# Second attention: row maxima two pairs ahead, row sums in adds of 1024 columns on GpSimd

## The reference, cut to what matters

```
k_in = v_in = layer_norm(ctx) * g + b            # ctx: 8 x 1601 x 128
q = rope(q_in @ Wq + bq);  k = rope(k_in @ Wk + bk);  v = v_in @ Wv + bv     # 16 heads of 64
scores = einsum("bhqd,bhkd->bhqk", q, k) / 8;  keys past the length: -inf
attn = softmax(scores, axis=-1);  out = einsum("bhqk,bhkd->bhqd", attn, v)
x = x + tanh(g_xattn[1]) * (out.reshape(8, 256, 1024) @ Wo + bo)
```

## Time and profile before

| what | us |
|---|---|
| median of 3 runs | 3376.14 |
| lowest and highest | 3375.39, 3378.19 |
| the profiled execution, its own time | 3378.97 |
| its span, first to last instruction | 3377.2 |
| PE busy | 2960.7 |
| DVE busy | 2171.2 |
| ACT busy | 1449.0 |
| POOL busy | 1340.0 |

### The profile page before, as it was taken

One profiled execution on the slowest core, in us unless ns is written; L12 is line 12 of the kernel. 1 busy time (PEld: TensorE's weight loads), 2 busy tenths in 40 slices (PEclk: granted clock), 3 DMA queues, 4 the chain that ended last, 5 costly groups with the idle time before them and its releaser, 6 DMA issues. The chain is left out here.

```text
span 3377.2 us, 81656 instructions
## 1 busy us (share of the span) xinstructions
PE 2960.7 (88%) x32026; PEld 1721.3 (51%) x32026; DVE 2171.2 (64%) x6576; ACT 1449.0 (43%) x2171; POOL 1340.0 (40%) x1205
## 2 busy tenths in 40 slices
PE   4599999999999367589899898998989989995998
PEld 3444444444444245356556565665656656663454
DVE  4366666665664544677777777777777777774343
ACT  2256656665665022244444444444444444441211
POOL 2000000000000000378778787877878878783000
PEclk8789999998998578699999999999999999997999
DMA  4400000000000000200000000000000000001000
GB/s 126 134 20 14 14 14 13 14 14 14 14 10 2 25 0 0 87 6 16 11 6 23 6 16 11 7 22 6 16 11 8 21 6 7 8 3 43 0 0 13
DMA packets 66728, 66.16 MB, mean 20 GB/s; under 512 B 8543, under 2 KB 60271, under 8 KB 65860
## 3 DMA queue, kind: packets, MB, share of 16 engines
q1 hardware_dynamic: 66372, 61.18, 6.3%
HBM read 53.23 MB, written 7.92 MB: 18 GB/s over the span
## 5 line engine op out<-in xcount | busy, mean ns | idle before, releaser
L1383 ACT ACTIVATE a_probs<-psS 128x1024 f32<-128x1024 f32 (+1 forms) x448 | 431.7, 964 | 777.5 <-PE psS L1280 777.5
L648 DVE CUSTOM_DVE_ANT_0 a_junk<-psT,a_mask 128x384 f16<-128x384 f32 (+1 forms) x1024 | 547.8, 574 | 332.2 <-PE psT L528 318.3
L610 ACT ACTIVATE a_probs<-psS 128x1024 f32<-128x1024 f32 (+2 forms) x512 | 442.5, 864 | 240.0 <-PE psS L553 240.0
L1679 POOL MEMSET a_shut<- 128x3328 f16 x1 | 2.9, 2872 | 1312.8 <-POOLq L1082 1312.8
L1673 POOL TENSOR_TENSOR a_acc<-a_acc,a_probs 128x512 f32<-128x512 f32 x320 | 408.2, 1276 | 274.7 <-ACT a_probs L1383 273.0
L1675 POOL TENSOR_TENSOR a_acc<-a_acc,a_probs 128x512 f32<-128x512 f32 x320 | 407.4, 1273 | 25.1
L1524 DVE CUSTOM_DVE_ANT_0 a_junk<-psS,a_mask 128x400 f16<-128x400 f32 (+1 forms) x512 | 273.6, 572 | 106.0 <-PE psS L1255 89.0
L1524 DVE CUSTOM_DVE_ANT_0 a_junk<-psT,a_mask 128x400 f16<-128x400 f32 (+1 forms) x512 | 273.6, 572 | 100.5 <-PE psT L1255 84.5
L564 PE MATMUL psO<-a_probs,a_values 128*9 128x256 f32 x3328 | 325.3, 393 | 0.5 <-ACT a_turned L622 0.5
L543 PE MATMUL psS<-a_mask_t,a_stack 128*64 128x256 f16 x3328 | 292.2, 290 | 0.0
L1647 POOL TENSOR_TENSOR a_klo<-a_kt,a_khi 128x400 f16<-128x400 f32 (+1 forms) x256 | 242.7, 948 | 9.9 <-ACT a_khi L1424 9.9
(11 more groups left out here) (308 smaller groups left out, 5736.9 us busy)
## 6 DMA issues: line engine op xcount, KB each, us to landing
a_wq<-in_wq SPq DMA_DIRECT2D x64, 128.0 KB, 2.1
a_kaug<-a_keys SPq DMA_DIRECT2D x288, 24.0 KB
a_keys<-p_kst SPq DMA_DIRECT2D x8, 832.0 KB, 4.7
p_ctx<-in_ctx SPq DMA_DIRECT2D x8, 768.0 KB
a_ctx<-in_ctx SPq DMA_DIRECT2D x8, 768.0 KB
a_mask<-a_pad SPq DMA_DIRECT2D x8, 400.2 KB
a_kaug<-a_keys SPq DMA_DIRECT2D x96, 32.0 KB
p_mask_raw<-in_mask_t SPq DMA_DIRECT2D x6, 448.0 KB, 6.2
```

The source lines that it names most:

```text
L610: nc.scalar.activation(dst, src, ACT.Exp).then_inc(exp_done, 1)
L648: nc.vector.tensor_tensor_reduce(junk[:, i % 2, 0:PIECE[j]], psA[i % 2][:, 0:PIECE[j]], mask[:, t, j, 0:PIECE[j]], 1.0, LOWEST, ALU.add, A ...
L1383: nc.scalar.activation(dst, src, ACT.Exp).then_inc(exp_done, 1)
```

## The change

- Row maxima are taken two pairs ahead: `ahead` and `row_max` are for pair `it + 2`, with `AHEAD1` = 2, 2, 1, 1, 1, 1, 0 units in the slots. `negative_max` is in slot 6, `turn_max` and `take_max` in slot 1 of the next iteration.
- The keys and the query go three pairs ahead (`it + 3`), so four pairs are kept (`KEPT1`), and there is one more iteration at the start.
- POOL keeps the slot's two chunks apart in an accumulator of 128 x 1024, and so adds a whole slot in one instruction: five adds of 1024 columns and one of 512 for a pair.
- `total` makes one column per head and block of 128 queries: 16 fp32 matmuls with 64 columns of the accumulator as the stationary operand and one column of ones as the moving one. They are a piece of the ring, `sums`. DVE takes the reciprocal of these four columns (`invert_sums`). `spread` in slot 4 spreads them over 64 rows by four matmuls with the identity, ACT copies the result to SBUF (`take_inverse`), and `divide` only multiplies, in slot 5.
- The statistics of a context are spread over the slots of the iteration before, the normalising is split into four groups in slots 1 to 4, the transposes are in slots 2 to 5. ACT makes the fp16 high part from PSUM, and DVE's `context_hi` is gone.
- `project` and `leave` stand behind `weigh`.

```diff
-AHEAD1 = [2, 2, 2, 2, 0, 0, 0]
+AHEAD1 = [2, 2, 1, 1, 1, 1, 0]
+KEPT1 = 4
 RING1 = 5
 VALUES1 = {2: (0, 1), 4: (2, 3)}
-ITERATIONS1 = range(-2, PAIRS1 + 1)
+ITERATIONS1 = range(-3, PAIRS1 + 1)
...
+        w.acc = sb("a1_acc", [P, 2, 4, T])
+        w.rec, w.inv = sb("a1_rec", [P, 2, 2, TT]), sb("a1_inv", [P, 2, T])
...
             def total(n):
-                pe.wait_ge(sum_done, SLOTS1 * (n + 1))
+                pe.wait_ge(sum_done, 6 * (n + 1))
+                out = piece(("sums", n))
                 for hd in range(2):
-                    ins = nc.tensor.matmul(w.sums[n % 2][64 * hd:64 * hd + 64, T:2 * T], m.ones[:, 0:64],
-                                           w.acc[:, n % 2, hd, :], start=True, stop=True, skip_group_check=True)
+                    for t in range(TT):
+                        for part in range(2):
+                            o = t * P + 64 * part
+                            for x in range(2):
+                                ins = nc.tensor.matmul(out[64 * part:64 * part + 64, hd * TT + t:hd * TT + t + 1],
+                                                       w.acc[:, n % 2, 2 * hd + x, o:o + 64], m.ones[:, 0:1],
+                                                       start=(hd == 0 and t == 0 and x == 0), stop=(x == 1),
+                                                       skip_group_check=True)
+                ins.then_inc(near_full, 1)
+
+            def spread(n):
+                pe.wait_ge(rec_done, n + 1)
+                for t in range(TT):
+                    for hd in range(2):
+                        ins = nc.tensor.matmul(w.sums[n % 2][64 * hd:64 * hd + 64, T + t * P:T + (t + 1) * P],
+                                               w.rec[:, n % 2, hd, t:t + 1].to_broadcast([P, 64]), m.ident[:, :],
+                                               start=False, stop=True, skip_group_check=True)
                 ins.then_inc(r_full, 1)
...
-                    if is_pair(it + 1):
+                    if is_pair(it + 2):
                         for u in units_ahead(sl):
                             for hd in range(2):
-                                ahead(it + 1, u, hd)
-                    if normed_in(it) is not None and 1 <= sl <= 4:
-                        turn(normed_in(it), sl - 1)
+                                ahead(it + 2, u, hd)
+                    if normed_in(it) is not None and 2 <= sl <= 5:
+                        turn(normed_in(it), sl - 2)
                     if is_pair(it + 1):
                         for v in VALUES1.get(sl, ()):
                             value(it + 1, v)
-                    if is_pair(it + 2) and sl == 3:
-                        query(it + 2)
-                    if is_pair(it + 2) and sl >= 3:
+                    if is_pair(it + 3) and sl == 3:
+                        query(it + 3)
+                    if is_pair(it + 3) and sl >= 3:
                         for part in range(2):
-                            key(it + 2, sl - 3, part)
-                    if leaves_in(it) is not None and sl == 5:
-                        project(leaves_in(it))
-                    if leaves_in(it) is not None and sl == 6:
-                        leave(leaves_in(it))
+                            key(it + 3, sl - 3, part)
+                    if is_pair(it + 1) and sl == 1:
+                        turn_max(it + 1)
                     if sl == 0 and is_pair(it - 1):
                         weigh(it - 1, SLOTS1 - 1)
                     if sl > 0 and is_pair(it):
                         weigh(it, sl - 1)
                     if sl == 3 and is_pair(it - 1):
                         total(it - 1)
-                    if sl == 5 and is_pair(it + 1):
-                        turn_max(it + 1)
+                    if sl == 4 and is_pair(it - 1):
+                        spread(it - 1)
+                    if leaves_in(it) is not None and sl == 5:
+                        project(leaves_in(it))
+                    if leaves_in(it) is not None and sl == 6:
+                        leave(leaves_in(it))
...
+                if nb >= 2:
+                    act.wait_ge(near_full, at["value", PER_BATCH * (nb - 1) - 1, 3] + 1)
+                nc.scalar.activation(w.chi[:, nb % 2, o:o + width], src[:, 0:width], ACT.Identity, bias=w.shift[:, :],
+                                     scale=w.gain[:, :]).then_inc(c_hi, 1)
...
+            def take_inverse(n):
+                act.wait_ge(r_full, n + 1)
+                if n >= 2:
+                    act.wait_ge(out_done, n - 1)
+                nc.scalar.copy(w.inv[:, n % 2, :], w.sums[n % 2][:, T:2 * T]).then_inc(r_taken, 1)
...
+            def normalise(nb, q):
                 dve.wait_ge(ln_step, 4 * nb + 4)
-                for c in range(SC):
+                for c in GROUPS[q]:
                     r = rows(c)
                     ins = nc.vector.tensor_scalar(w.ctx[0:r, c, :], w.ctx[0:r, c, :], w.mv[0:r, c, 0:1],
                                                   w.rstd[0:r, c:c + 1], ALU.subtract, ALU.mult)
                 ins.then_inc(ln_normed, 1)
...
+            def invert_sums(n):
+                src = take(("sums", n))
+                if n >= 2:
+                    dve.wait_ge(r_full, n - 1)
+                nc.vector.reciprocal(w.rec[:, n % 2, :, :].rearrange("p h t -> p (h t)"), src[:, 0:2 * TT]
+                                     ).then_inc(rec_done, 1)
+                dve.wait_ge(rec_done, n + 1)
+                dve.sem_inc(near_free[bank_of(("sums", n))], 1)
+
             def divide(n):
                 b, p = n // PER_BATCH, n % PER_BATCH
-                dve.wait_ge(r_full, n + 1)
-                if n > 0:
-                    dve.wait_ge(out_done, n)
-                nc.vector.reciprocal(w.rec[:, :], w.sums[n % 2][:, T:2 * T]).then_inc(rec_done, 1)
-                dve.wait_ge(rec_done, n + 1)
+                dve.wait_ge(r_taken, n + 1)
                 if p == 0 and b > 0:
                     dve.wait_ge(near_full, at["project", b - 1] + 1)
-                nc.vector.tensor_tensor(w.outs[:, p, :], w.sums[n % 2][:, 0:T], w.rec[:, :],
+                nc.vector.tensor_tensor(w.outs[:, p, :], w.sums[n % 2][:, 0:T], w.inv[:, n % 2, :],
                                         ALU.mult).then_inc(out_done, 1)
...
                 for sl in range(SLOTS1):
-                    if sl == 4 and is_pair(it + 1):
-                        negative_max(it + 1)
-                    if is_pair(it + 1):
+                    if is_pair(it + 2):
                         for u in units_ahead(sl):
                             for hd in range(2):
-                                row_max(it + 1, u, hd)
-                    if is_pair(it + 2) and sl == 3:
-                        rotate_query(it + 2)
-                    if is_pair(it + 2) and sl >= 3:
-                        rotate(it + 2, sl - 3)
-                    if it % PER_BATCH == 1 and normed_in(it + 1) is not None and sl == 6:
-                        statistics(normed_in(it + 1))
+                                row_max(it + 2, u, hd)
+                    if is_pair(it + 2) and sl == 6:
+                        negative_max(it + 2)
+                    if it >= 0 and normed_in(it + 1) is not None:
+                        statistics(normed_in(it + 1), slot_chunks(sl))
+                        if sl == SLOTS1 - 1:
+                            variance(normed_in(it + 1))
                     if normed_in(it) is not None and sl == 0:
-                        normalise(normed_in(it))
-                    if normed_in(it) is not None and 2 <= sl <= 5:
-                        context_hi(normed_in(it), sl - 2)
+                        inverse(normed_in(it))
+                    if normed_in(it) is not None and 1 <= sl <= 4:
+                        normalise(normed_in(it), sl - 1)
+                    if is_pair(it + 3) and sl == 3:
+                        rotate_query(it + 3)
+                    if is_pair(it + 3) and sl >= 3:
+                        rotate(it + 3, sl - 3)
                     if sl == 3 and is_pair(it - 1):
+                        invert_sums(it - 1)
+                    if sl == 5 and is_pair(it - 1):
                         divide(it - 1)
...
+                if sl == 1:
                     if n >= 2:
-                        pool.wait_ge(r_full, n - 1)
-                    nc.gpsimd.tensor_tensor(acc, src[:, :, 0, :], src[:, :, 1, :], ALU.add).then_inc(sum_done, 1)
+                        pool.wait_ge(near_full, at["sums", n - 2] + 1)
+                    nc.gpsimd.tensor_tensor(acc, w.probs[:, (k - 1) % RING1, :, :], src, ALU.add).then_inc(sum_done, 1)
                     return
-                pool.wait_ge(sum_done, k)
+                pool.wait_ge(sum_done, 6 * n + sl - 1)
                 if sl < SLOTS1 - 1:
-                    nc.gpsimd.tensor_tensor(acc, acc, src[:, :, 0, :], ALU.add).then_inc(sum_step, 1)
-                    pool.wait_ge(sum_step, 5 * n + sl)
```

(48 more changed lines are left out.)

107 lines of the change are left out of this document (52 added, 55 removed).

## The result

The kernel after takes 3409.72 us (median of 4 runs, 3404.78 to 3413.14), the one before 3377.16 us in the same comparison: ratio 1.0091, 95% interval 1.0077 to 1.0104. Slower by 0.9%; the forecast was 3427 in a range of 3325 to 3505. The side is right. The sum behind it is not: its three largest terms (1, 2 and 5) were wrong, the first in the opposite direction to the other two.

What follows compares the result with a forecast made beforehand. TensorE was taken as the bound, with waits at the batch boundary and small ones in steady pairs. 3379.0 - 45 + 42 + 8 + 10 + 36 = 3430, less 2.8 for the median: 3427 us, range 3325 to 3505.

Steps and rivals of the forecast that it cites:

- Term 1: Batch boundary: normalising in quarters saves 6.4 of 14.4 us in each of seven pairs, -45 us.
- one long add per group: Batch boundary, Term 1: each group of four normalising instructions on DVE meets one long POOL add.
- Term 2: Row sums on PE: 1.7 us of passes, less waits gone, net +0.70 us per pair, +42 us.
- One changeover more and a short wait for its bank, 0.15: In Term 2: an extra PE changeover and the transposed maximum's wait for its bank cost 0.15 us per pair.
- Engines that aren't the bound: In Term 2: DVE's 1.5 us saved per pair and POOL's savings are on engines that don't bound the kernel.
- Term 5: Clock: it falls behind the new sums as behind the first attention's groups, 0.6 us per pair, +36 us.
- I am wrong if the sums take 1.2 us or less: Sign against the forecast: sums of 1.2 us or less per pair, or steady pairs shorter than 23.9.
- Term 3: Projection: PE waits about 1.2 us for the last divide, moved to DVE's slot 5, eight times, +8 us.
- Term 4: Ends of the stage: one more iteration ahead of the first scores, partly offset, +10 us.
- The sums are cheap: Rival, 25%: 32 passes take about 1.0 us, too short for the clock to fall; faster, 3349 us.
- DVE becomes the bound at the boundary: Rival, 5%: each normalising instruction waits for a long add, 27 us in a pair, nothing won there; 3472 us.

Runs made afterwards that it cites:

- e13: Kernel before with only the normalising in quarters (double conversion on ScalarE, four pairs of keys and projection behind the weighing came along), old sums, one pair ahead: 3327.99 us.
- e6: Kernel after with the maximum pass one pair ahead again, new sums and normalising in quarters kept: 3419.19 us.
- e3: Kernel after with the row sums of before (adds of 512, two matmuls against ones, 256-column reciprocal and divide in slot 3): 3424.34 us.
- e10: Kernel after with the 13 normalising instructions moved from DVE to ScalarE, same slots: 3365.47 us.
- e15: Kernel after with each of GpSimd's five adds of 1024 columns issued as two of 512: 3408.89 us.
- e4: Kernel after with the 32 passes of the sums issued twice, same result: 3457.46 us.
- e1: Kernel after with the maximum's transposes one slot later (slot 2 for slot 1): 3378.66 us.
- e5: Kernel before with the new row sums alone, divide in slot 5: 3466.01 us.
- e11: Kernel after with maximum's transposes in slot 2, normalising on ScalarE, variance behind the last rotation and divide at the head of slot 5: 3315.11 us.
- e2: Kernel after with the normalising in another instruction form (two operands from memory, inverse deviation broadcast), same count and place: 3415.13 us.

## Why the prediction was right, and where it was not

Plain pair and time of the four ways to combine sums and lead, all with the quarters:

| | old sums | new sums |
|---|---|---|
| maximum one pair ahead | 23.94, 3328 (e13) | 24.86, 3419 (e6) |
| maximum two pairs ahead | 24.75, 3424 (e3) | 24.25, 3410 (after) |

Each part alone loses 0.8 to 0.9 us per pair; together they lose 0.3. The waits of PE in a plain pair show why: with one pair ahead they are 1.0 us whichever the sums (0.5 for the values, 0.5 for the query); with two ahead they are 1.9 with the old sums (e3), whose reciprocal stands in DVE's full slot 3, and 0.4 with the new. That interaction is what a sum of terms could not hold.

**Term 1 (-45): the step that failed.** Measured -13.9, and -2.0 a pair where I had 6.4 saved. By itself the step was right: the quarters alone take 37.87 to 31.3, 6.6 saved (e13). In the kernel after, 4.6 of it went back. Shown: DVE is held by POOL (5.3 us for a group of four), TensorE waits 4.2 us for it at the first transpose, and the pairs fall to 30.1 when the normalising leaves DVE (e10). The "one long add per group" of the prediction was too few: the group of the long pair meets two and a subtraction. But the add's width is not the cause (e15), nor is the time that DVE spends on the 13 instructions: 9.0 us in e13, 9.2 in e3 and 9.3 in e15, in pairs of 31, 39 and 36 us. The excess of these pairs over a plain one is 7.3 us in e13, 11.1 with the new sums (e6), 12.5 with the early maximum (e3), 11.6 with both. Here is the longest pair of e3, with the same 290 instructions of PE as the pair of e13 above:

```profile
2124.39:2163.79 39.40, 31.05 (x290) 18.31 (x290) 29.38 (x79) 18.52 (x28) 22.45 (x21) 0.83 0.02 5
```

Of the 8.9 us between them 5.8 are busy time of PE, at a clock of 0.83 and not 1.00, and 3.1 are idle time. The clock is 0.95 to 1.00 in the seven pairs of e13, 0.90 to 0.91 in e6's and 0.83 to 0.90 in e3's. Why each of the two parts, neither of which touches the normalising, adds 4 to 5 us of idle time and low clock stays open.

**Term 2 (+42, +0.70 per pair).** The passes take

```profile
1714.12 1.10 PE L1325 MATMUL psS<-ones,a_acc 128*64 128x1 f32 x32
1715.15 0.28 PE L1288 MATMUL psS<-a_qhi,a_khi 64*128 64x256 f16 x2
```

1.03 us and not 1.7: the lower end of my bounds, 0.029 us per pass (e4). I had gone by the difference of two loads' durations, but in the profile loads of 0.137 us start 0.03 us apart, so their durations are no spacing. "One changeover more and a short wait for its bank, 0.15" had a size of 0.64 (e1). The waits for values and query did go, by the early maximum and not by DVE's saved time (e5 has them still). "Engines that aren't the bound" was wrong of DVE: with the early maximum its 2.2 us in slot 3 are worth 1.3 us of PE (e3). Measured +0.33 a pair (PE's busy time 22.87 to 23.80, its idle time 1.05 to 0.44), +20 in all.

**Term 5 (+36): nothing.** The clock is 1.00 in all plain pairs, and in those with a group twice as long (e4). I carried a habit of the first attention over. What separates the two stages isn't shown: PE is busy all the time in the first attention's intervals too, 27.47 of 27.47 us at the full clock and 30.42 of 30.42 where it fell.

Terms 2 and 5 together were 58 us too high, Term 1 31 too optimistic. That 3427 is near 3410 is luck, and so is the side: with Term 1 at its forecast -45 and the others as measured (+20, 0, +10, +12) the sum is -3, no change. By the prediction's own sign, "I am wrong if the sums take 1.2 us or less", its mechanism was wrong: they take 1.03.

**Term 3 (+8).** 1.45 us more than in a plain pair's own growth, seven times: +10. The wait stands in the trace of after, 1.6 us where I had 1.2, and it is gone in e11:

```profile
PE psT L1344 <- DVE a_outs L1626: 1.6, 1, 1.6
```

**Term 4 (+10).** +17.8 at the start and -6 at the end (-3.7, where seven plain pairs grow by 2.3): +12. e6 shows that the start is the second iteration (85.0 us without it).

**The rivals.** "The sums are cheap" had the sums right, 1.03 us and no fall of the clock, and the time wrong, since it kept Term 1's 45 us. "DVE becomes the bound at the boundary", given 5% and 3472, came nearest to the real loss, but with 27 us for the 13 instructions, where DVE spends 10.0 and 11.6 on them in the short and the long pair: it is busy 28 to 30 of 33 to 38 us there. Its "nothing is won there" came true in e1.

## What to carry to other kernels

Price a step that moves instructions by what stands ahead of them in its new slot on every engine that touches its banks, not by the engine's mean load: the same 2.2 us cost 0.5 us per pair in slot 3 and left no wait in slot 2 (with the maximum's transposes moved too), and one slot for four transposes was worth 31 us. Look at the durations of DVE's instructions between operands in SBUF while GpSimd works there; where they are held as here, try ScalarE, which did the same work beside GpSimd without a hold and won 44 us. When a change has several parts, run each alone: the quarters alone were worth 1.5%, and the change that contained them lost 0.9%.

## What was not expected of the hardware

- A two-operand instruction of DVE with all operands in SBUF is held by GpSimd as the one-operand form is (5.47 us for four, e2), and ScalarE is not (1.64 us for four, none over 0.51, e10).
- With GpSimd's adds split in two, a group of four is held to 3.98 us in place of 5.3, and the pairs are no shorter in the mean, 35.9 (e15).
- A stream of fp32 passes with 64 stationary columns and one moving column runs at 0.03 us per pass (1.03 us for 32, 0.93 for 32 more), and with 64 of them in a plain pair its granted clock stayed at 1.00 (e4).
